# List writes of a routed transformer layer on one core: pairs in two turns, or single writes spread over seven and paced by ScalarE

## The reference

```python
topk_w, topk_idx = jax.lax.top_k(gates, TOP_K)                 # two experts per row
norm_w = topk_w / (jnp.sum(topk_w, axis=-1, keepdims=True) + 1e-08)
flat_e = topk_idx.reshape(-1)
onehot = (flat_e[:, None] == jnp.arange(NUM_EXPERTS)[None, :])
pos_all = jnp.cumsum(onehot, axis=0) - 1                       # place of a row in its expert's list
valid = position < capacity                                    # 1280 places for each expert
buf = buf.at[flat_e, pos_scatter].set(x_flat[flat_t], mode='drop')
h = jnp.maximum(jnp.einsum('ecd,edh->ech', buf, w1) + b1[:, None, :], 0.0)
out_e = jnp.einsum('ech,ehd->ecd', h, w2) + b2[:, None, :]
out_flat = jnp.zeros_like(x_flat).at[flat_t].add(gathered * w_eff[:, None])
```

## Time and profile before

| | |
|---|---|
| median of 3 runs | 821.34 us (819.98 to 822.44) |
| span of the profiled execution | 856.8 us (the profile gives no other time of that execution) |
| busy: PE, DVE, ACT, POOL | 784.5 (92%), 605.1 (71%), 442.1 (52%), 410.2 us (48%) |
| list writes on POOL (line 533) | 64, 65.5 us, 1023 ns each |
| attention stage, and experts after it | about 360 us, and the rest |

### The profile page before, as it was taken

The page is one execution under the profiler, slowest core; times in us unless marked ns, Lnnn a source line. Parts: engine busy times, 40 slices in busy tenths (PEclk is TensorE's granted clock), DMA queues, the critical chain, the costliest instruction groups (busy, mean ns, idle before and its releaser), DMA issues.

```text
span 856.8 us, 16628 instructions
## 1 busy us (share of the span) xinstructions
PE 784.5 (92%) x5919; PEld 648.5 (76%) x5919; DVE 605.1 (71%) x1325; ACT 442.1 (52%) x753; POOL 410.2 (48%) x595
## 2 busy tenths in 40 slices
PE   7699989999989985896999999999999999999994
PEld 7577766677667653585889898898898888988993
DVE  5768878888888885683756856756657568665983
ACT  3166757777666664542534534534345345443670
POOL 1011245555555546457146445254364462556675
PEclk9799999999999998799899999999999999999998
DMA  5677765555555572326145245253352451533741
GB/s 158 135 165 161 161 153 113 114 113 114 116 114 110 115 141 73 116 51 180 20 91 109 41 89 115 43 130 50 81 111 40 96 112 31 140 57 57 288 179 46
DMA packets 71534, 92.75 MB, mean 108 GB/s; under 512 B 12972, under 2 KB 55885, under 8 KB 71324
## 3 DMA queue, kind: packets, MB, share of 16 engines
q1 hardware_dynamic: 53308, 67.95, 31.0%
q0 software_dynamic: 16928, 22.15, 14.9%
q10 hardware_dynamic: 1216, 1.57, 0.8%
HBM read 39.18 MB, written 26.89 MB: 77 GB/s over the span
## 4 chain that ended last, share of the span: by engine, by line
PE 69%; DVE 14%; issue 5%; POOL 3%; another core or an unknown queue 3%; DMA 2%; ACT 2%; ACTq 1%; POOLq 0%; DVEq 0%; SPq 0%
PE bank L1718 14%; DVE negm L890 10%; PE wide L1687 8%; PE wide L1685 8%; PE wide L1686 8%; PE bank L985 7%; PE bank L1720 7%; PE wide L1030 5%; PE bank L1664 2%; PE wide L1048 2%; PE bank L1095 2%; PE bank L1064 1%; PE bank L994 1%; POOL slot_list L533 1%
## 5 line engine op out<-in xcount | busy, mean ns | idle before, releaser
L1359 POOL DMA_INDIRECT acc_rows<-o_w,lists x70 | 120.4, 1720 | 181.6 <-ACT o_w L1508 167.9
L890 DVE TENSOR_REDUCE negm<-wide 128x4 f32<-128x1024 f32 x128 | 156.1, 1222 | 50.5 <-PE wide L1030 31.7
L630 ACT ACTIVATE probs<-wide 128x1024 f32<-128x1024 f32 x128 | 131.0, 1024 | 89.1 <-PE wide L1048 68.9
L1475 ACT ACTIVATE h<-wide,b1T 128x512 f32<-128x512 f32 (+1 forms) x200 | 115.0, 600 | 96.8 <-PE wide L1687 69.1
L1720 PE MATMUL bank<-stack,h_lo 128*128 128x256 f32 x560 | 156.9, 280 | 0.0
L1685 PE MATMUL wide<-g_hi,stack 128*128 128x512 f32 (+1 forms) x400 | 140.8, 352 | 5.2 <-DVE g_lo L1536 4.1
L1687 PE MATMUL wide<-g_hi,stack 128*128 128x512 f32 (+1 forms) x400 | 140.1, 350 | 0.1
L1686 PE MATMUL wide<-g_lo,stack 128*128 128x512 f32 (+1 forms) x400 | 140.1, 350 | 0.0
L1508 ACT ACTIVATE o_w<-o_b,lists 128x256 f32<-128x256 f32 x70 | 35.7, 510 | 148.6 <-DVE o_b L1646 135.5
L1718 PE MATMUL bank<-stack,h_hi 128*128 128x512 f32 x304 | 108.7, 401 | 1.3 <-DVE o_b L1646 1.3
L1720 PEld LDWEIGHTS bank<-stack,h_lo 128*128 128x128 f32 x560 | 105.6, 189 | 0.0
(11 more groups left out here) (211 smaller groups left out, 1640.9 us busy)
## 6 DMA issues: line engine op xcount, KB each, us to landing
stack<-qk SPq DMA_DIRECT2D x180, 128.0 KB, 4.2
w_raw<-in_L_ffn_w SPq DMA_DIRECT2D x16, 1024.0 KB
x_sb<-in_L_attn_x SPq DMA_DIRECT2D x16, 256.0 KB, 5.1
x_rows<-x SPq DMA_DIRECT2D x16, 256.0 KB
acc_rows<-x SPq DMA_DIRECT2D x16, 256.0 KB
acc_sb<-acc_rows SPq DMA_DIRECT2D x8, 512.0 KB, 11.1
out<-acc_sb SPq DMA_DIRECT2D x8, 512.0 KB
x_rows<-zrow SPq DMA_DIRECT2D x2, 1152.0 KB, 6.6
```

Of the source, the lines that this page charges most:

```text
L630: nc.scalar.activation(probs[:, i % 4].rearrange("p x c t -> p x (c t)"), shifted_banks(i)[:, :, :], ACT.Exp, scale=SCALE).then_inc(exp_do ...
L890: nc.vector.tensor_reduce(negm[n % 2][:, :, :, u].rearrange("p c x -> p x c"), score_banks(PAIRS * n + u)[:, :, :].rearrange("p x (c t) -> ...
L1359: nc.gpsimd.indirect_dma_start(out=acc_d, out_offset=bass.IndirectOffsetOnAxis(ap=lists[:, e, QC * c + r, 0:1], axis=0), in_=o_w[c][:, r, ...
L1475: ins = nc.scalar.activation(h[u % 2][:, t], banks[BZ[u % 4]][:, t], ACT.Relu, bias=b1T[:, FT * e + f:FT * e + f + 1])
```

## The change

The four writes of a sequence become single steps with turns of their own. For the first 12 sequences they are due at turns 51, 53, 55 and 57 in place of 51, 51, 52 and 52. Ahead of each write POOL waits until ACT has finished the exponential of the turn before (while there are exponentials left). Sequence 12 is written at turns 46, 48, 50 and 51 (before: 46, 46, 47, 47), so that its writes and those of sequence 11 (turns 139, 141, 143, 145) fall on one a turn between turns 141 and 147; sequence 13 at turns 30, 31, 33 and 33 after turn 120 (before: all at 33), its writes now standing behind the gathers in the loop; sequences 14 and 15 keep their turns. `LAST` keeps its value of 167.

```diff
--- before.py
+++ after.py
@@ -303,8 +303,10 @@
         UT, AT, O, LIST = 34, 36, 38, 50
         LN, LG, PICK, SEEN, EX = (40, 40, 40, 40), (41, 41, 41, 41), (43, 43, 43, 42), (44, 43, 43, 42), (45, 44, 45, 43)
         X1, STORE, POS, SLOT = (42, 46, 45, 44), (48, 48, 48, 45), (46, 44, 45, 43), (47, 45, 45, 44)
-        ENTRY, WRITE = (48, 45, 45, 44), ((51, 46, 46, 45), (52, 47, 50, 46))
-        LAST = 8 * (NB - 1) + WRITE[1][3] + 1
+        ENTRY = (48, 45, 45, 44)
+        WRITE = ((51, 46, 46, 45), (53, 48, 46, 45), (55, 50, 50, 46), (57, 51, 50, 46))
+        FIRST_WRITE = (30, 31, 33, 33)
+        LAST = 8 * (NB - 1) + WRITE[3][3] + 1
         LTAIL = NB - 4
         EARLY, FIRST = g["EARLY"], NB - LATE
         END = 8 * (NB - 1)
@@ -523,17 +525,19 @@
                 pool.wait_ge(token_done, m + 1)
                 nc.gpsimd.tensor_scalar(tok[:, :], tok[:, :], float(S), None, ALU.add).then_inc(tok_done, 1)
 
-            def into_lists(m, c):
-                if m == 0 and c == 0:
+            def into_list(m, part, turn):
+                if m == 0 and part == 0:
                     pool.wait_ge(filled, 80)
                 pool.wait_ge(dest_done, m + 1)
                 pool.wait_ge(token_done, m + 1)
                 pool.wait_ge(weight_done, m + 1)
-                for k in range(TOPK):
-                    nc.gpsimd.indirect_dma_start(
-                        out=list_d, out_offset=bass.IndirectOffsetOnAxis(ap=dest[m % 4][:, c, k:k + 1], axis=0),
-                        in_=item[m % 4][:, c, k, :], in_offset=None, bounds_check=NE * CAP - 1,
-                        oob_is_err=False).then_inc(listed[m % 4], 16)
+                if turn - ST0 <= PAIRS * NB:
+                    pool.wait_ge(exp_done, turn - ST0)
+                c, k = divmod(part, TOPK)
+                nc.gpsimd.indirect_dma_start(
+                    out=list_d, out_offset=bass.IndirectOffsetOnAxis(ap=dest[m % 4][:, c, k:k + 1], axis=0),
+                    in_=item[m % 4][:, c, k, :], in_offset=None, bounds_check=NE * CAP - 1,
+                    oob_is_err=False).then_inc(listed[m % 4], 16)
 
             for turn in range(LAST + 1):
                 n = due(turn, XT, NB)
@@ -561,18 +565,19 @@
                 m = due(turn, LIST, LTAIL)
                 if m is not None:
                     entries(m)
-                for c in range(QC):
-                    m = routed(turn, WRITE[c])
+                for part in range(QC * TOPK):
+                    m = routed(turn, WRITE[part])
                     if m is not None and m != FIRST:
-                        into_lists(m, c)
-                    if turn == END - 8 + LN[0] + 1:
-                        into_lists(FIRST, c)
+                        into_list(m, part, turn)
                 if turn == END + PV0 + 4:
                     pool.wait_ge(v_ready, QC * NB)
                     pool.wait_ge(g["list0_loaded"], 16)
                     gather(0, 0)
                     pool.wait_ge(g["list1_loaded"], 16)
                     gather(0, 1)
+                for part in range(QC * TOPK):
+                    if turn == END + FIRST_WRITE[part]:
+                        into_list(FIRST, part, turn)
 
         def scalar_program(act, rows_hi, relu):
             def w2_part(i):
```

## The result

The changed kernel takes 829.72 us (829.02 to 830.6, four runs), the kernel before 821.52 (819.98 to 822.44, four runs): 1.0111 times as long, with a 95% interval from 1.0092 to 1.0131. That is 8.2 us slower, where 799 us and a gain were forecast. And yet the profiled span fell from 856.8 to 827.3 us.

A forecast was written before the change was run, and what follows sets the result against it. Runs of POOL's list writes were taken to hold back PE's signals. Gains of 17.4 in steady sequences and 7.9 at the end, less 2.2, made 23.1 of 856.8 us, 2.7%, so 799 us from 821.34; range 793 to 818.

The forecast's parts named there:

- What bounds the kernel now: Attention stage: runs of POOL's list writes hold back PE's signals, from about the third write until 1.3 us after the last.
- Sum: Whole kernel: 17.4 - 2.2 + 7.9 = 23.1 us of the profiled 856.8, carried over as 2.7% to 799 us.
- 17.4 for the sequences: Steady sequences of the attention stage: removing the runs of four writes gains 17.4 us, between nothing and 18.2.
- 10.4 for the end: End of the attention stage: spreading eight writes gains 8.8 us of stall and 1.6 of clock, before 2.5 is taken off.
- The last line of the prediction's tests: Whole kernel: the forecast fails altogether if the span falls by 23 us and the timed runs don't.
- The signs of right: Profile after: sequences about 18.8 us, no unnamed wait, ACT idle at most some 3 us at the end, clock near 1.
- the sign of "slower": Profile after, end of stage: transposes of the first gathered rows wait for a DMA longer than today.
- What is left of it, and the added waits: Steady sequences: a remaining close pair costs 0.2 us in each of 11, 2.2 in all; the added waits cost nothing.
- the push: POOL: the fourth write pushes the next sequence's arithmetic back by 1.4 us, at no cost.
- Sequence 13: Two of its four writes move ahead of POOL's normalisation of sequence 14, where POOL waits; effect nothing.
- Nothing comes of it: Rival, whole kernel: writes cost the same anywhere, the stall isn't POOL's, or exists only under profiling; 821 us, chance 0.11.
- Slower: Rival, end of stage: paced writes delay the second chunk's rows, some 3 us on top; 824 us, chance 0.08.

The follow-up runs named there:

- e0: The kernel before, unchanged, profiled a second time: span 819.0 us, 1.8 us under the 820.79 that this execution took.
- e1: Against the changed kernel: single paced writes only for sequences 0 to 10; sequences 11, 12 and 13 written as before. 822.45 us, 1.0025 to the kernel before.
- e2: The changed kernel without the wait on exponentials, every write keeping its new turn: 830.86 us, 1.0112 to the kernel before.
- e7: The kernel before with only sequence 13's writes at the places of the changed kernel: 820.36 us, 0.9988.
- e5: The kernel before with sequence 11's fourth write moved from turn 140 to 145, behind sequence 12's four and the normalisation: 828.59 us, 1.0097.
- e11: The changed kernel with the 1 MB load of second biases issued at turn 161 in place of 152: 825.45 us, 1.0069 to the kernel before.
- e4: The changed kernel, waits kept, with sequence 11's last write and sequence 12's last two due at turn 144, ahead of the normalisation: 825.91 us, 1.0063 to the kernel before.
- e10: Profile of the changed kernel with sequence 11's four writes first and all eight ahead of the normalisation, waits kept; this kernel was timed at 822.89 us, 1.0033.

## Why the prediction was wrong

*What bounds the kernel now.* The times were read rightly, but they belong to that execution, and the mechanism put on them, that a run of list writes holds back what PE signals from its third write on, fails in e0: the same runs hold back nothing. Its own warning stands in the sum: what is longest in a profiled run need not be as long in the others. It was given 0.11 inside a rival, because onset with the first write and restarts after the last looked like cause and effect. They may be, in that execution, and no run shows why it stood still; in e0 nothing does.

*Sum*: this is the step that failed. 23.1 us of an 856.8 us span were carried over as a share of 821.34. But 35.5 us of that span are in no timed run, and the 23.1 are a part of just these. The true credit was nothing: 17.4 for the sequences measured 0 (18.6 us with and without runs of four), 10.4 for the end measured 0. The last line of the prediction's tests, a span that falls while the timed runs don't, is what came: it fell by 29.5.

*The signs of right* mostly showed: sequences of 18.63, no unnamed wait, no idling of ACT above 0.68 us among the last exponentials. These three show in the kernel before as well (e0), so they couldn't speak for the change. The clock was at 1.00 up to 331.25 and at 0.50 from 337.20 on, and the sign of "slower", first gathered rows that wait for a DMA, showed with 4.84 us.

*What is left of it, and the added waits*: the push, put at 1.4 us, was 1.8, and its price of nothing wrong by 2 us (e1), because sequence 11's writes do wait for that arithmetic, the gathers for them, and PE for the gathers, which land late. The waits at nothing were right (e2). *Sequence 13* at nothing was right (e7).

*The rivals.* "Nothing comes of it" came near the right reason with the last of its three, a stall that is there only while a profile is taken: the timed runs don't have it, though the later profiles don't either. "Slower" had the right place and chain, lists to gathers to the first gathered rows, and the wrong write, cause and size. It took the second list's last write, 2.6 us late through pacing, and priced it at some 3. It was the first list's last write, 9.2 us later (315.06 to 324.25), mostly through its place behind two of sequence 12's writes and the normalisation. A reader of the turns could have seen that: sequence 12's writes at 142 and 144 come ahead of 145, and in turn 145 the normalisation stands first in the loop. Two more terms were missing, the slower landing and the clock after PE's idling. And its slack was taken from the stalled profile, 10 us; in e0 the first gathered rows are used about 2.5 us after they land (the second gather starts at 325.68, lands 3.0 later, and PE takes them at 331.20). At 0.08 the rival that came true was far too cheap.

## What to carry to other kernels

Hold a profiled span against the timed runs before costing anything by its rows: where it is 4% too long, the stalls in it may be the 4%, and a gain from removing them is no gain. When a step is moved by turns, list what else its engine does in the turns that it passes, and which transfers the last one releases; one write that came to stand behind four others and a short normalisation cost 7.7 us here (e5), and the pacing, which looked dangerous, nothing that could be told.

## What the runs showed that was not expected

The stall of the first profile, some 29 us over the attention stage (its last exponential started at 356.19, against 326.94 in e0), came back in no later profile, though the writes ran just as close; what released the waiting engines is open. The gathers landed later where a large load went out among them: 5.2 us in the median with the 1 MB load there, 3.0 with it moved away (e11). And a wait of 2.33 us (e4) was followed by a granted clock of 0.50, while after waits of 1.90 (e1) and 1.45 (e10) it was 1.00.
